# The first half of a two-block adaLN kernel's first layer in another order, with products of ones on TensorE and the attention update in fp32r over high and low parts

## What is computed

```python
mod = (silu(L0_c) @ L0_wmod).reshape(4, 6, 1, 512)
sa, ca, ga, sb, cb, gb = mod[:, 0..5]
ga = (2 * (ga >= 0) - 1) * maximum(abs(ga), 0.25)      # gb too
h = layernorm(x) * (1 + ca) + sa
# q: 16 x 32 heads, k and v: 16; o is the same for all 32 heads
scores = einsum('bsdh,bse->bsde', q, k) / 4            # 16 x 16 for each row
o = einsum('bsde,bse->bsd', softmax(scores), v)        # 16 numbers for each row
x = x + ga * broadcast(o, 32 heads)
h = layernorm(x) * (1 + cb) + sb
x = x + gb * where(query_sel & row_sel, h @ weight.T + bias, 0)
```

## Time and profile before

| | |
|---|---|
| median of 3 runs | 1827.91 us |
| the profiled execution | 1824.19 us, its span 1822.4 us |
| PE busy | 1791.6 us (98%) |
| PE weight loads busy | 1491.9 us (82%) |
| DVE busy | 1264.5 us (69%) |
| ACT busy | 1096.5 us (60%) |
| POOL busy | 440.2 us (24%) |
| HBM traffic | 181 GB/s over the span |
| chain that ended last | PE 92%, DVE 4%, ACT 2% |

### The profile page before, as it was taken

One profiled execution on the slowest core, in us unless ns is written; L12 is line 12 of the kernel. 1 busy time (PEld: TensorE's weight loads), 2 busy tenths in 40 slices (PEclk: granted clock), 3 DMA queues, 4 the chain that ended last, 5 costly groups with the idle time before them and its releaser, 6 DMA issues.

```text
span 1822.4 us, 29016 instructions
## 1 busy us (share of the span) xinstructions
PE 1791.6 (98%) x8847; PEld 1491.9 (82%) x8847; DVE 1264.5 (69%) x2980; ACT 1096.5 (60%) x2650; POOL 440.2 (24%) x434
## 2 busy tenths in 40 slices
PE   7899999999999999999999999999999999999999
PEld 5466788888888888888888888888888878888887
DVE  4788677787867776767776776767777786544533
ACT  4585765666667666766666666767676664342331
POOL 1324223041413233241413122240303132011000
PEclk9799999999999999999999999999999999999999
DMA  9024767676776758686777868677777777313110
GB/s 345 9 70 151 225 190 209 201 221 179 213 209 197 215 179 230 183 242 206 229 208 214 230 183 233 187 226 199 216 208 216 232 185 276 99 47 115 36 34 24
DMA packets 240424, 331.25 MB, mean 182 GB/s; under 512 B 26040, under 2 KB 165560, under 8 KB 239936
## 3 DMA queue, kind: packets, MB, share of 16 engines
q1 hardware_dynamic: 239792, 328.93, 60.7%
q10 hardware_dynamic: 528, 1.05, 0.1%
HBM read 200.39 MB, written 129.50 MB: 181 GB/s over the span
## 4 chain that ended last, share of the span: by engine, by line
PE 92%; DVE 4%; ACT 2%; issue 1%; SPq 1%; DMA 0%; POOL 0%; DVEq 0%; ACTq 0%; POOLq 0%
PE ps L2202 28%; PE ps L2272 19%; PE ps L2255 12%; PE ps L2395 11%; PE ps L2238 10%; PE ps L2380 5%; PE ps L2235 1%; PE ps L120 1%; PE ps L1326 1%; PE ps L1213 1%; PE ps L1293 1%; PE ps L1254 1%; DVE pd L2808 0%; PE ps L1220 0%; ACT xh L605 0%
## 5 line engine op out<-in xcount | busy, mean ns | idle before, releaser
L2202 PE MATMUL ps<-hA,wq 128*128 128x512 f32 x1536 | 378.2, 395 | 0.0
L2272 PE MATMUL ps<-wo,oT 128*128 128x512 f32 x1536 | 366.3, 389 | 0.2 <-DVE acc L2824 0.2
L2272 PEld LDWEIGHTS ps<-wo,oT 128*128 128x128 f32 x1536 | 288.1, 188 | 60.1 <-issue 0.4
L2549 ACT ACTIVATE pt<-pd 128x1280 fp32r<-128x1280 f32 x128 | 163.0, 1273 | 272.0 <-PE ps L2255 235.7
L2202 PEld LDWEIGHTS ps<-hA,wq 128*128 128x128 f32 x1536 | 279.5, 188 | 53.7
L2780 DVE CUSTOM_DVE_ANT_0 ps<-ps,mask 128x384 f32<-128x384 f32 (+7 forms) x512 | 220.7, 484 | 140.8 <-PE ps L2238 137.4
L2531 ACT ACTIVATE probs<-ps,nmax 128x384 f32<-128x384 f32 (+7 forms) x512 | 250.1, 504 | 60.0 <-DVE nmax L2780 57.2
L2539 ACT ACTIVATE probs<-probs,rinv 128x384 f32<-128x384 f32 (+7 forms) x512 | 232.5, 525 | 46.7 <-DVE rinv L2791 46.7
L2800 DVE STREAM_TRANSPOSE tp<-probs 128x384 f32<-128x384 f32 (+3 forms) x512 | 215.4, 477 | 4.4 <-ACT probs L2539 4.4
L2255 PE MATMUL ps<-pt,V 128*128 128x256 f32 (+1 forms) x896 | 216.2, 329 | 1.5 <-DVE pd L2808 0.6
L2808 DVE TENSOR_TENSOR pd<-pd,pt 128x1280 fp32r<-128x1280 f32 x128 | 193.6, 1512 | 1.9 <-ACT pt L2549 1.9
(11 more groups left out here) (280 smaller groups left out, 2758.0 us busy)
## 6 DMA issues: line engine op xcount, KB each, us to landing
turned_blocks<-tp SPq DMA_DIRECT2D x128, 640.0 KB, 3.4
pd<-turned_blocks SPq DMA_DIRECT2D x512, 160.0 KB, 3.5
wq_next<-in_L_attn_w_q_dram SPq DMA_DIRECT2D x16, 1024.0 KB, 7.2
wo_in<-in_L_attn_w_o_dram SPq DMA_DIRECT2D x15, 1024.0 KB, 9.5
turned_weights<-hf_chunk SPq DMA_DIRECT2D x168, 64.0 KB, 2.8
turned_values<-tv SPq DMA_DIRECT2D x32, 256.0 KB, 4.3
xh_m<-turned_weights SPq DMA_DIRECT2D x28, 256.0 KB, 3.7
wm<-in_L_wmod_dram SPq DMA_DIRECT2D x4, 1024.0 KB, 10.0
```

Source lines behind the costliest of these rows:

```text
L2202: last = nc.tensor.matmul(ps[:, bank, :], w[i][:, c, cols], hT[k][:, c, b * S:(b + 1) * S], start=(c == 0 and n == 0), stop=(c == DC - 1 a ...
L2272: last = nc.tensor.matmul(ps[:, bank, :], oT[x_][:, b, h, AT[r] * P:(AT[r] + 1) * P], wo[y_][:, h, :], start=(h == 0 and n == 0), stop=(h ...
L2549: nc.scalar.activation(flat(pt[:]), flat(pd[:, u % 2].bitcast(F32)), ACT.Copy).then_inc(phi_done, 1)
```

## The change

- **Loads.** The centroids, the linear's weights, its bias and the assignments come before the half of wmod for mod 3 and before X[2]. mod 1 waits for its own load (`ld_sa`) and no longer for the biases behind it.
- **Order.** `columns1(0)`, `sum_weights` and `project(0)` come before what needs mod 1; mod 3 is made after the linear's weights are turned; half of the transposes of X[2] come before `turn_o(0)`; `statistics1(1)` comes before the gate ga; `exponentials(1)`, `take_mod(5)` and `root1(2)` before `normal2(0)`.
- **Products of ones.** 41 products of a 128x512 tile of ones (`warm`), 128 rows deep and in fp32r, stand in eight places of PE's list. Nothing reads their results.
- **The update.** o is written as four parts of 16 columns: rounded to fp32r, the rest, rounded, and zeros in the last; ga's columns in G are two parts rounded, two parts the rest. One fp32r product 64 rows deep takes the place of one fp32 product 16 rows deep. `turn_o` makes two transposes, `copy_o` copies 256 columns, `outputs` has two more DVE instructions, `spread_gate` two POOL instructions of 256 columns in place of one of 512, and the gate two more of DVE.

```diff
@@ first_sync
                 load_x(1)
                 load_one(2)
-                load_x(2)
-                load_one(3)
                 sp.dma_start(cen_in[:], cent).then_inc(ld_at_first, 16)
...
+                load_one(3)
+                load_x(2)
                 load_wm(2)
...
@@ mod_loaded
-                return {0: (ld_wm[0], 16), 1: (ld_b, 64), 2: (ld_wm[1], 16), 3: (ld_at_first, 48)} \
+                return {0: (ld_wm[0], 16), 1: (ld_sa, 16), 2: (ld_wm[1], 16), 3: (ld_at_first, 80)} \
@@ spread_gate
-                    gate = mod[0][:, DC * MOD_GA:DC * MOD_GA + DC, b:b + 1].to_broadcast([P, DC, P])
-                    nc.gpsimd.tensor_tensor(spread[:, b], place[:].rearrange("p c t e -> p c (t e)"), gate, ALU.mult) \
-                        .then_inc(spread_done, 1)
+                    for k in range(2):
+                        gate = gate_parts[:, k, :, b:b + 1].bitcast(F32).rearrange("p c (o e) -> p c o e", o=1) \
+                            .to_broadcast([P, DC, 2, 2 * E0])
+                        last = nc.gpsimd.tensor_tensor(parts(spread[:, b])[:, :, :, k],
+                                                       parts(place[:].rearrange("p c t e -> p c (t e)"))[:, :, :, k], gate, ALU.mult)
@@ outputs
-                    nc.vector.tensor_tensor(o_t[:, :, 0:E0], by_tile(2), by_tile(1), ALU.mult).then_inc(o_done, 1)
+                    link(nc.vector.tensor_tensor(red[:, 2], red[:, 2], red[:, 1], ALU.mult))
...
+                    link(nc.vector.tensor_copy(by_part[:, :, 0:3:2, :], twice))
+                    nc.vector.tensor_tensor(o_t[:, :, E0:2 * E0], by_tile, o_t[:, :, 0:E0].bitcast(F32), ALU.subtract).then_inc(o_done, 1)
@@ first_tensor
+                def keep_busy(n, bank):
+                    for _ in range(n):
+                        nc.tensor.matmul(ps[:, bank, :], warm[:, 0:P], warm[:], start=True, stop=True)
+                pe.wait_ge(wcat_done, WARM_SET)
+                keep_busy(6, BANK_P)
...
@@ update
-                        at = slice(QB * t, QB * t + E0)
-                        nc.tensor.matmul(ps[:, BANK_U + t % 2, :], oT_[at, :], G[at, b, :], start=True, stop=True).then_inc(upd_ps, 1)
+                        at = slice(OR * (t % 2), OR * (t % 2) + OR)
+                        nc.tensor.matmul(ps[:, BANK_U + t % 2, :], oT_[at, t // 2, :], G[at, b, :], start=True, stop=True).then_inc(upd_ps, 1)
```

More of the change, by code:

```diff
@@ L269, in adaln_two_blocks @@
             with ExitStack() as early:
-                place = sb(early, "place", [P, DC, TB, P // TB], F32)
+                place = sb(early, "place", [P, DC, P // E0, E0], F32)
                 bias_hi = sb(early, "bias_hi", [ROW_LO + 1, D], F32R)
@@ L697, in first_scalar @@
                 take_mod(2)
+                exponentials(0)
                 copy_columns1(1)
-                copy_mod(3)
-                exponentials(0)
-                take_mod(3)
                 root1(1)
-                copy_rows(0)
                 copy_weights(0)
                 copy_weights(1)
+                copy_rows(0)
                 copy_centroids()
@@ L708, in first_scalar @@
                 copy_weights(3)
+                columns_of(2, range(2))
                 copy_o(0)
-                copy_mod(4)
-                round_bias()
[L712 to L720, removed]
+                columns_of(2, range(2, 4))
+                copy_mod(3)
+                copy_columns1(2)
+                take_mod(3)
+                exponentials(1)
+                copy_mod(4)
+                copy_rows(1)
+                copy_rows(2)
+                root2(0)
+                take_mod(4)
+                copy_rows(3)
+                copy_mod(5)
+                root1(2)
+                round_bias()
+                take_mod(5)
                 normal2(0)
-                take_mod(5)
-                columns_of(2, range(1, 4))
                 whole(0, range(1))
@@ L1048, in mods @@
                     mods_finish(link, layer, first, end, tmp_g)
+                    if (layer, first) == (0, MOD_GA):
+                        gate = mod[0][:, DC * MOD_GA:DC * MOD_GA + DC, :]
+                        link(nc.vector.tensor_copy(gate_parts[:, 0], gate))
+                        link(nc.vector.tensor_tensor(gate_parts[:, 1], gate, gate_parts[:, 0].bitcast(F32), ALU.subtract))
                     dve.sem_inc(mods_done, 1)
@@ L1073, in first_vector @@
                 scores(0)
+                statistics1(1)
                 mods(3, 0, MOD_GA, MOD_SB)
@@ L1284, in turn_o @@
                     pe.wait_ge(o_done, b + 1)
-                    nc.tensor.transpose(ps[:, BANK_U + 1, 0:P], o_t[:].rearrange("p t e -> p (t e)"), ident[:]).then_inc(ot_ps, 1)
+                    for k in range(2):
+                        last = nc.tensor.transpose(ps[:, BANK_U + 1, k * P:(k + 1) * P],
+                                                   o_t[:, 2 * k:2 * k + 2].rearrange("p t e -> p (t e)").bitcast(F32), ident[:])
+                    last.then_inc(ot_ps, 1)
                 def update(b, tiles):
@@ L1385, in first_tensor @@
                 turn_weights(3)
+                turn(1, 2, range(2))
+                keep_busy(6, BANK_U + 1)
                 turn_o(0)
                 pe.wait_ge(rows_sb, 1)
+                keep_busy(3, BANK_U)
                 update(0, range(2))
-                pe.wait_ge(wf_done, 3)
+                turn(1, 2, range(2, 4))
+                pe.wait_ge(wf_done, 4)
+                make_mod(pe, 3)
+                update(0, range(2, TB))
+                columns1(2)
+                turn_mod(pe, 3)
                 make_mod(pe, 4)
-                update(0, range(2, TB))
-                turn(1, 2, range(2))
-                turn_mod(pe, 4)
                 pe.wait_ge(x1_done, 4)
@@ L1414, in first_tensor @@
                 update(1, range(2))
-                turn_mod(pe, 7)
                 update(1, range(2, TB))
```

96 lines of the change are left out of this document (51 added, 45 removed).

## The result

The changed kernel took 1818.75 us (median of 4 runs, 1816.25 to 1819.16), the kernel before, beside it, 1828.33 us. The ratio is 0.9947, with a 95% interval of 0.9934 to 0.9960: 9.6 us faster, where 1813 us and about 14 were forecast.

The account below looks back on a forecast made before the run. Early bound: PE at low clock, then DVE and ACT from 39 to 67 us. Terms 4.9 + 3.0 - 0.5 + 3.6 + 1.7 + 1.2 + 0.5 = 14.4 us off the 1827.91 median gave 1813 us, range 1804 to 1823.

Parts of the forecast that it names:

- rival A: PE's clock falls between mod 1's product and the offsets' end and after: only 9.8 us gained, 1818 us; chance 16%.
- Start to `fold`: From the start to DVE taking the offsets of batches 1 to 3, at 34.0 in place of 38.88: 4.9 us gained.
- `statistics1(1)`: On DVE, moved from between `fold` and `outputs(0)` to beside PE's offsets, 28.7 to 31.7 us: 3.0 us gained.
- `outputs`: DVE's added copy and subtraction cost 0.55 us more per batch, 0.5 us lost up to `shift` of batch 0.
- ACT ahead of `normal2(0)`: ACT's work between `shift` and `normal2(0)` moves ahead, leaving 0.9 us in place of 4.56: 3.6 us gained, bounds 1.5 and 4.6.
- To `whole(0)`: From `normal2(0)` to `whole(0)`, 2.69 us become 1.0 as copies have moved and transposes run at high clock: 1.7 us gained.
- The table load: ACT's 1.28 us table load at `root1(3)` goes, the square root's table being loaded already: 1.2 us gained.
- The update: A pair takes 0.46 us, 0.6 less; batches 0 and 1 count nothing, 2 and 3 give 0.5 us, ends -1.1 and 2.4.
- The ones: 41 products in PE's waits, 9 to 19 us of its time, covered by other waits: costed at 0, at worst 2.6.
- Loads: X[2] loads behind 2.5 MB more, 6 us; what its transposes wait beside `outputs(0)` is covered: nothing lost.
- Rival B: The second norm's gain is given back as DVE runs late within 88 to 140 us: 6 to 8 lost, 1820; chance 14%.
- C: Slower than before: a new gap on PE lets the clock fall and stay low; 36 us of it give 1831; chance 4%.

Follow-up runs that it names:

- The later ones: The changed kernel with 22 more products of ones in PE's waits between 51 and 76 us: 1811.7 us, ratio 0.9916.

## Why the prediction was right, and where it was not

The time lies in the range and on the forecast side, at two thirds of the gain. It lies nearest to rival A's 1818 us. One thing holds for all items below. They compare single traces, and the same lists don't take the same time twice: in the nine traces of the changed order, with and without early ones and with either update, `outputs(0)` starts between 33.7 and 36.5 us, with X[1]'s transposes at high clock in five of them, in part in one, and at low clock in three. By its items:

1. *Start to `fold`*: 4.0 us for 4.9. The load off the path is right, 3.2 us at `columns1(0)`; X[1]'s transposes ran at low clock in this execution (3.28 us). In the five with high clock they took 2.5 us, and `outputs(0)` started at 33.7 to 34.4 us, for the 34.6 of the walk: the step is right, and which clock it meets varies. The ten ones ahead of `columns1(0)` don't bring its high clock, since it is there without them.
2. *`statistics1(1)`* stood in its cover, 28.92 to 31.9 us. 3.0 as forecast.
3. *`outputs`* has three instructions in place of its last one, 0.55 us each while POOL was at work, and 0.22 each in batch 1, when it wasn't; 0.6 of loss for 0.5.
4. *ACT ahead of `normal2(0)`* failed: 3.6 us forecast, nothing gained in this execution. `normal2(0)` waited 4.8 us behind `shift`, against 4.6 before. The walk had mod 5's vector ready at 55.6 us, with PE at high clock and not held by mod 4's copy. It came at 60.8, by way of 1.1 us of wait for a copy that stands behind the exponentials, and of three steps of PE at low clock. The later ones show the clock's share: the same steps in 1 us each, a wait of 2.0 us for 4.8, and 7 us at the end. What is left, 2.0 for the 0.9 of the walk, is the order's. In the two traces of this order with the old update the clock fell at 58 us in place of 54, and the wait was 2.4 us.
5. *To `whole(0)`*: 1.3 us in place of 2.7, so 1.4 for 1.7. From there to `columns2(0)`, which no item counts, 0.8 us was lost, at low clock.
6. *The table load* went from `root1(3)`, and `dots(0)` is 7.5 us earlier where `columns2(0)` was 6.8: 0.7 for 1.2; `columns2(0)` itself took 1.0 us more, at low clock.
7. *The update* is mis-sized. A pair takes 0.49 us, as forecast (0.46), and in the two traces batches 2 and 3 give nothing (7.5 us at `dots(0)`, 7.4 at `dots(3)`). But in the medians it is worth 2.8 us on top of order and ones, 3.7 on top of the order, and 5.4 alone, for 0.5. The walk weighed only a pair's own time. The traces of the old update have a stretch at low clock behind `dots(0)` in two of six, of 14 and 6 us, the eight of the new one none of over 4 us. That this is how the update gains, and in which batches, is likely and not shown.
8. *The ones* cost nothing beside the order, as said, and gave nothing, which was not said.
9. *Loads* held up nothing.

The sum took high clock in items 1, 4 and 5 for granted. No row of before shows it for X[1]'s transposes (3.43 us, at low clock) or from 47 to 64 us; that is rival A, which came in part and at a later place than A put it. Rival B did not come, nor C. Measured against the sum: item 4 is 3.6 short or more, items 1, 5 and 6 together 1.7, and item 7 gives more than its 0.5 in the medians. So part of the agreement is luck: what the update gave beyond its term made up for some of what item 4 lacked.

Of the signs named in advance, `columns1(0)` by 17 us, `outputs(0)` right behind `fold`, and pairs of updates under 0.6 us at high clock came. `fold` stood at 35.25 us for 35. `normal2(0)` by 57 us (60.88) and `columns2(0)` by 72 us (76.67) did not come, and from `columns2(0)` to the end the span was 1.3 us longer and not 1 to 3 shorter.

What stays open: where the executions of 1828 us spend their time, and whether the shallow update causes it. That products 16 rows deep don't hold the clock as those of 128 do is shown for ones only. Why the same lists meet another clock from one execution to the next is open too.

## What to carry to other kernels

When an engine's clock depends on its work, a walk along the path must say at which clock each step runs, and from which row; where two lists wait for one another in short steps, a row at low clock gives twice the time in each. Filling products paid where the waits end in PE's own steps on the path (7 us here), and gave nothing in the waits before 44 us; in the order of before, what they won was lost again in a low stretch behind them. So try them with the stretch in view and not by count. And take several executions before trusting one trace for a few microseconds: the one of before was 4 us quicker than its median, and `outputs(0)` moved by up to 2.8 us between traces with the same lists up to it.

## What the runs showed of the hardware

**Busy alone did not hold the clock; the depth of the products made a difference.** With 22 products of 512 columns and 128 rows PE was at 1.00 from 54 to 82 us; with the same ones 16 rows deep it was busy 7.00 of each 7 us from 61 us on and at 0.50, 0.53 in the last of the three (the windows of the two kernels, above). The mean clock over the span was 0.997 or 0.998 in six executions with deep ones and 0.991 to 0.996 in ten with shallow ones. The Trainium skill, TensorE: Matmul & The Clock Gate, Part 1: The HAM clock gate, ties the gate to how busy PE has been of late; the trace agrees for the deep products and not for the shallow ones.

**The clock came up while PE did nothing but transposes.** In the trace of before it fell as X[1]'s 16 transposes began (26.6 to 30.2 us), and was back at their end:

```profile
26.00:27.00 1.00, 1.00 (x9) 1.00 (x9) 0.15 (x2) 0.00 (x0) 0.00 (x0) 0.75 1.03 381
29.00:30.00 1.00, 1.00 (x7) 0.89 (x5) 1.00 (x1) 0.59 (x2) 0.00 (x0) 0.54 1.08 393
30.00:31.00 1.00, 1.00 (x10) 0.16 (x8) 0.96 (x2) 0.76 (x2) 0.00 (x0) 1.00 1.06 404
```

In the changed kernel it fell at 23 us, in the offsets' products; the 16 transposes are PE's only work from 24.0 to 27.2 us, and the clock is back before their end:

```profile
24.00:25.00 1.00, 1.00 (x6) 1.00 (x6) 0.77 (x5) 0.00 (x0) 0.00 (x0) 0.50 1.02 377
26.00:27.00 1.00, 1.00 (x8) 0.92 (x7) 0.96 (x2) 0.71 (x2) 0.00 (x0) 0.74 1.09 277
27.00:28.00 1.00, 1.00 (x11) 0.16 (x8) 0.97 (x2) 0.90 (x2) 0.00 (x0) 1.00 1.02 262
```

Transposes run at the high clock as well: the 16 of X[0] took 1.94 us in the changed kernel and 3.65 us before. The Trainium skill, TensorE: Matmul & The Clock Gate, Part 4: PE-mode transpose, says that the full rate doesn't engage for transposes, since they don't count as busy in the same way. The two traces differ from that, and the measurement decides.
